# Gathers, scatters and weight subtractions of the GpSimd queue in another order, in an expert stage on one core

## The chip, the cores and the metric

The kernel runs on one core of one Trainium2 chip. The metric is the device time of one execution in microseconds (us); the median of three runs is quoted. Engines are named as in the profile: PE (TensorE, products), DVE (VectorE), ACT (ScalarE), POOL (GpSimd) and SP (SyncE, which only issues DMAs here).

## The reference

A block of a decoder: cross attention of 2048 tokens (8 x 256, width 256) over 120 context rows each, gated and added, then a mixture of 8 experts where each token goes to the one expert with the highest router logit.

```python
x = x + tanh(g_xattn) * xattn(layernorm(x), ctx)          # softmax attention
h = layernorm(x)                                           # (8, 256, 256)
e_of = argmax(h @ router_w.T, axis=-1)
for e in range(8):                                         # I = 704
    mask = (e_of == e)[..., None]
    xe = where(mask, h, 0)
    ye = (silu(xe @ gate_w[e].T) * (xe @ up_w[e].T)) @ down_w[e].T
    out = out + where(mask, ye, 0)
x = x + tanh(g_ffn) * out
```

## The kernel before

It has two stages. The first (to about 72 us) does the attention for eight batches, writes the rows to a table in DRAM (`x1_rows`), routes every token and sorts the tokens by expert. The second is the expert stage. For expert j the tokens' rows are fetched by indirect DMAs (gathers) into a seat in SBUF, in blocks of 128 tokens: two full blocks always (`FULL` = 2), a third block of 80 only if the expert has more than 256 tokens. Here experts 1, 3, 5 and 6 have a third block. After the work the result rows are sent by indirect DMAs (scatters) to their places in `out`. There are five seats and gathers run two experts ahead (`AHEAD` = 2).

Weights are float32 and each product is done in three passes with numbers split in a high and a low part. SP loads the raw weights (`load_gu` L436 for gate and up, `load_d` L443 for down). ACT makes the high part (L728, called by `split_gu` L854 and `split_d` L861). POOL subtracts it from the raw weights to get the low part: `low_gu` (L521) with one L528 for each of two halves c = 0 and 1 and one L529 for a tail, and `low_d` (L531) with one L537. `low_gu(j)` waits for ACT's split of expert j (`a_hg`) and ends in the signal `p_lg`, `low_d(j)` in `p_ld`. SP's next load into the same room (two rooms of raw weights) waits for `p_lg` or `p_ld`, and PE waits for `p_lg` before an expert's first product and for `p_ld` before its down products.

PE does for expert j: six chunks q of gate and up products (L1147, a half chunk first), then transposes the next expert's tokens (L1125), then the down products (L1180). For each chunk ACT takes the gate product and makes the silu (L839, L841), DVE multiplies it with the up product (L1460, L1462), ACT makes the high part (L850, L852) and DVE the low part (L1469, L1471). The up product of chunk q waits for the low part of chunk q - 3 of the same bank, and that stands on DVE behind the multiplication of the next chunk (L1460), which waits for PE's signal of that chunk's up product. ACT normalises gathered rows (L815) and copies PE's transposes (L823). DVE adds a finished block of the output to its seat (L1482, signals `v_out`, `v_out3`), which a scatter waits for.

The order of POOL's queue is written out by hand. `gather(j)` (L604) issues the two full blocks (`fetch`, L578), reads the token count of expert j and issues the third block under a condition; `scatter(j)` (L617) does the same with `send` (L587). Two gathers stand ahead of `low_gu(2)` and `low_d(2)`; then each round j issues `gather(j + 2)`, `low_gu(j + 2)`, `low_d(j + 2)` and `scatter(j - 1)` (L624 to L636). Since `scatter(j - 1)` ends one round and `gather(j + 3)` begins the next, four to six indirect DMAs stand next to each other.

Of the kernel before, what the change touches and what calls it, by code (L numbers as in the profile page):

```python
# [24 lines left out]
F32 = mybir.dt.float32  # L25
# [4 lines left out]
ALU = mybir.AluOpType  # L30
# [7 lines left out]
E, I = 8, 704  # L38
C = H // P
# [8 lines left out]
SPLIT = 3  # L48
# [7 lines left out]
FULL = BL - 1  # L56
# [4 lines left out]
SEATS = 5  # L61
AHEAD = 2
# [7 lines left out]
def flamingo_moe(nc, x, ctxT, g_x, g_f, WqT, WkT, Wv, bv, WrT, Wgu, Wd, WdL, out):  # L70
    with ExitStack() as stack:
# [108 lines left out]
        def raw_of(j, c):  # L180

            return raw_gu[:, j % RAW, 2 * I * c:2 * I * (c + 1)].rearrange("p (o s n) -> p s o n", o=2, s=2)
# [5 lines left out]
        def halves(j, w_part, c):  # L188

            start = start_of(j, w_part, c)  # L190
            both_sides = wgu[:, start:start + 2 * SIDE].rearrange("p (s i) -> p s i", s=2)
            return both_sides[:, :, 0:I].rearrange("p s (o n) -> p s o n", o=2)

        def tails(j, w_part):

            start = start_of(j, w_part, 0)
            return wgu[:, start:start + C * ROW].rearrange("p (c n) -> p c n", c=C)[:, :, I:SIDE]

        def raw_tails(j):

            return raw_gu[:, j % RAW].rearrange("p (c n) -> p c n", c=C)[:, :, 2 * I - LAST:2 * I]
# [74 lines left out]
        a_hg, a_hd = sem("a_hg"), sem("a_hd")  # L276
        p_lg, p_ld = sem("p_lg"), sem("p_ld")
# [220 lines left out]
        def _(pool):  # L498
# [19 lines left out]
            pool.iota(iota_t[:].rearrange("p a b -> p (a b)"), pattern=[[1, NTOK]], base=-NTOK, channel_multiplier=0, **fl).then_inc(k_pool, 1)  # L518
            pool.iota(bounds[:].rearrange("p a b -> p (a b)"), pattern=[[G, MORE]], base=G, channel_multiplier=0, **fl).then_inc(k_pool, 1)

            def low_gu(j, pieces):  # L521

                pool.wait_ge(a_hg, j + 1)
                for c in range(C):
                    raw, hi, lo = raw_of(j, c), halves(j, 0, c), halves(j, 1, c)
                    for n in range(pieces):
                        where = (slice(None), n // 2, n % 2) if pieces > 1 else slice(None)
                        pool.tensor_tensor(lo[where], raw[where], hi[where].bitcast(F32), ALU.subtract)  # L528
                pool.tensor_tensor(tails(j, 1), raw_tails(j), tails(j, 0).bitcast(F32), ALU.subtract).then_inc(p_lg, 1)  # L529

            def low_d(j, pieces):  # L531

# [68 lines left out]
                    third(pool, "pool", sizes[r], lambda: pool.wait_ge(d_scat[r], 16 * BL),  # L601
                          lambda: pool.wait_ge(d_scat[r], 16 * FULL))

            def gather(j):  # L604

                r = j % SEATS
                if j >= SEATS:
                    third(pool, "pool", sizes[j - SEATS], lambda: pool.wait_ge(d_scat[r], 16 * BL),
                          lambda: pool.wait_ge(d_scat[r], 16 * FULL))
                for k in range(FULL):  # L610
                    fetch(j, k, d_gath[r][k])
                if j == 0:
                    pool.wait_ge(v_used, 1)
                sizes.append(count(pool, j))
                third(pool, "pool", sizes[j], lambda: fetch(j, FULL, d_rest[r]))

            def scatter(j):  # L617

                for k in range(FULL):
                    send(j, k, d_scat[j % SEATS])  # L620
                third(pool, "pool", sizes[j], lambda: send(j, FULL, d_scat[j % SEATS]))

            sizes = []
            for j in range(AHEAD):  # L624
                gather(j)
            low_gu(SPLIT - 1, 1)
            low_d(SPLIT - 1, 1)
            for j in range(E):
                if j + AHEAD < E:
                    gather(j + AHEAD)  # L630
                if SPLIT <= j + AHEAD < E:
                    low_gu(j + AHEAD, 1)
                    low_d(j + AHEAD, 1)
                if j:
                    scatter(j - 1)
            scatter(E - 1)  # L636


            def run(j):
# [961 lines left out]
```

## Time and profile before

| | us |
|---|---|
| median of three runs | 213.82 (213.01 to 213.95) |
| profiled execution, span from first to last instruction | 217.2 |
| PE busy | 190.9 |
| POOL busy | 134.8 |
| ACT busy | 116.1 |
| DVE busy | 112.6 |
| mean granted clock of PE over the span | 0.913 |

The profiled execution is one run of its own. A row of a timeline has the start of an instruction in us from the start of the span, its duration, the engine, the line of the kernel, the operation, what it writes and reads, how many instructions are merged in it, and in brackets how long its engine sat idle before and what ended that. A row in which several instructions are merged covers short gaps between them.

### The profile page before, as it was taken

What the parts mean: (1) busy time and instruction counts of PE and PEld (TensorE: products, weight loads), DVE (VectorE), ACT (ScalarE), POOL (GpSimd) and SP (SyncE); (2) the same over time, 40 slices, a digit from 0 to 9 for tenths busy, and PEclk for the clock granted to TensorE, in tenths of its full rate; (3) what the DMA queues carried; (4) which work ended last, traced back from release to release, by engine and by line L of the source; (5) the groups of instructions that cost most, each with busy time, mean ns of one, the idle gap of its engine ahead of it and who ended that gap; (6) DMA issues with size and microseconds to landing.
All of it is one profiled execution on the core that took longest, in us unless ns stands there. A gap on an engine that the chain in (4) does not pass through costs nothing.

```text
span 217.2 us, 4417 instructions
## 1 busy us (share of the span) xinstructions
PE 190.9 (88%) x1365; PEld 173.5 (80%) x1365; DVE 112.6 (52%) x362; ACT 116.1 (53%) x260; POOL 134.8 (62%) x140
## 2 busy tenths in 40 slices
PE   7899999996869697949999998699899699999980
PEld 3566899985668287949999997699799699899970
DVE  2588899976347413623654651551572552563640
ACT  1377778765137123636973984653796740641510
POOL 3002717959354589834998988998987996203111
PEclk9999999998558757997999999799999879999996
DMA  6999451394530126940095185067001101100001
GB/s 180 342 373 394 178 194 49 88 349 172 185 132 0 40 75 177 368 129 0 5 325 187 28 291 200 14 251 255 20 3 65 50 3 67 34 3 27 28 6 49
DMA packets 11710, 28.98 MB, mean 133 GB/s; under 512 B 1928, under 2 KB 8537, under 8 KB 10646
## 3 DMA queue, kind: packets, MB, share of 16 engines
q1 hardware_dynamic: 6320, 20.20, 26.8%
q0 software_dynamic: 1920, 4.53, 6.5%
q10 hardware_dynamic: 3430, 3.74, 4.9%
q8 instruction: 23, 0.38, 0.7%
q14 instruction: 17, 0.14, 0.2%
HBM read 24.26 MB, written 4.52 MB: 132 GB/s over the span
## 4 chain that ended last, share of the span: by engine, by line
PE 76%; DVE 7%; issue 4%; ACT 4%; DMA 4%; another core or an unknown queue 2%; ACTq 1%; POOL 0%; DVEq 0%; POOLq 0%
PE ps L1147 30%; PE ps L1180 19%; PE ps L1008 4%; DMA both<-in_ctxT 4%; PE ps L1029 3%; PE ps L947 3%; PE ps L988 3%; PE ps L977 3%; PE ps L1018 2%; PE ps L1113 2%; PE ps L1098 2%; PE ps L968 2%; PE ps L1125 1%; DVE ps L1460 1%
## 5 line engine op out<-in xcount | busy, mean ns | idle before, releaser
L1147 PE MATMUL ps<-xhT,wgu 128*128 128x256 f32 (+2 forms) x528 | 74.1, 301 | 7.5 <-DVE hT L1471 4.9
L1147 PEld LDWEIGHTS ps<-xhT,wgu 128*128 128x128 f32 x528 | 71.3, 200 | 9.7 <-DVE hT L1471 5.6
L528 POOL TENSOR_TENSOR wgu<-raw_gu,wgu 128x352 fp32r<-128x352 f32 (+1 forms) x28 | 52.8, 1917 | 14.4 <-ACT wgu L728 14.3
L1180 PE MATMUL ps<-wd,hT 128*128 128x256 f32 (+1 forms) x340 | 44.1, 289 | 3.0 <-DVE hT L1469 3.0
L1180 PEld LDWEIGHTS ps<-wd,hT 128*128 128x128 f32 (+1 forms) x340 | 42.3, 187 | 3.5 <-DVE hT L1469 3.4
L1460 DVE TENSOR_TENSOR ps<-V,ps 128x336 f32<-128x336 f32 x40 | 20.4, 511 | 33.8 <-PE ps L1147 24.0
L587 POOL DMA_INDIRECT out<-xin,table x20 | 19.6, 982 | 26.8 <-DVE xin L1482 23.3
L537 POOL TENSOR_TENSOR wd<-both,wd 128x512 fp32r<-128x512 f32 (+1 forms) x12 | 28.6, 2396 | 2.3 <-ACT wd L728 2.3
L839 ACT ACTIVATE V<-ps 128x336 f32<-128x336 f32 x40 | 17.9, 448 | 19.8 <-PE ps L1147 19.5
L578 POOL DMA_INDIRECT xin<-x_rows,table x20 | 19.5, 977 | 9.9 <-issue 5.6
L728 ACT ACTIVATE wgu<-raw_gu 128x704 fp32r<-128x704 f32 (+2 forms) x34 | 24.0, 771 | 1.2 <-issue 1.2
L1482 DVE SCALAR_TENSOR_TENSOR xin<-ps,tg,xin 128x256 f32<-128x256 f32 (+1 forms) x20 | 9.0, 480 | 27.3 <-PE ps L1180 25.1
L1469 DVE TENSOR_TENSOR hT<-ps,hT 128x336 fp32r<-128x336 f32 x40 | 20.0, 501 | 0.4
L850 ACT ACTIVATE hT<-ps 128x336 fp32r<-128x336 f32 x40 | 17.8, 446 | 0.8 <-DVE ps L1460 0.5
L841 ACT ACTIVATE V<-ps 64x336 f32<-64x336 f32 x8 | 3.5, 443 | 26.0 <-PE ps L1147 26.0
L815 ACT ACTIVATE A<-xin,stat 128x256 f32<-128x256 f32 (+1 forms) x20 | 11.8, 594 | 6.3 <-issue 6.3
L396 POOL TENSOR_TENSOR nwt<-nwt 128x8 f32<-128x8 f32 (+1 forms) x6 | 1.4, 232 | 21.9 <-DVE nwt L390 21.6
L728 ACT ACTIVATE wd<-both 128x768 fp32r<-128x768 f32 (+1 forms) x13 | 12.8, 988 | 0.5 <-DMA both<-in_WdL 0.5
L1029 PEld LDWEIGHTS ps<-wrc,wkT 128*128 128x128 f32 x64 | 9.4, 225 | 3.6 <-ACT wkT L725 3.6
L1029 PE MATMUL ps<-wrc,wkT 128*128 128x8 f32 x64 | 10.0, 284 | 1.4 <-ACT wkT L725 1.4
L1008 PE MATMUL ps<-V,pT 120*128 120x256 f32 x32 | 9.4, 420 | 1.8 <-ACT pT L719 1.8
L725 ACT ACTIVATE wkT<-ps 128x512 f32<-128x512 f32 x8 | 4.8, 599 | 11.2 <-PE ps L1018 11.2
(148 smaller groups left out, 248.2 us busy)
## 6 DMA issues: line engine op xcount, KB each, us to landing
raw_gu<-in_Wgu SPq DMA_DIRECT2D x8, 1408.0 KB, 8.6
both<-in_Wd SPq DMA_DIRECT2D x8, 640.0 KB, 4.3
x_rows<-x ACTq DMA_DIRECT2D x8, 256.0 KB, 3.5
xin<-in_x SPq DMA_DIRECT2D x7, 256.0 KB, 9.5
both<-in_WdL SPq DMA_DIRECT2D x16, 64.0 KB, 4.3
both<-in_ctxT ACTq DMA_DIRECT2D x2, 480.0 KB, 8.4
xin<-x_rows,table POOLq DMA_INDIRECT x20, 3.0
out<-xin,table POOLq DMA_INDIRECT x20
```

What stands on the lines that cost most here:

```text
L528: pool.tensor_tensor(lo[where], raw[where], hi[where].bitcast(F32), ALU.subtract)
L537: ins = pool.tensor_tensor(wd[:, j % SPLIT, some, 1, :], raw[:, some, :], wd[:, j % SPLIT, some, 0, :].bitcast(F32), ALU.subtract)
L578: pool.indirect_dma_start(out=seat(j, k), out_offset=None, in_=rows, in_offset=bass.IndirectOffsetOnAxis(ap=index(j, k), axis=0)).then_inc ...
L587: pool.indirect_dma_start(out=out, out_offset=bass.IndirectOffsetOnAxis(ap=index(j, k), axis=0), in_=seat(j, k), in_offset=None, bounds_ch ...
L728: return act.activation(dst, src, ACT.Copy)
L839: act.activation(sg[:, q % 2, :], ps[:, gate_bank(q), 0:G], ACT.Silu).then_inc(a_sg, 1)
L1008: last = pe.matmul(ps[:, 4, H * k:H * k + H], pT[:, P * k:P * k + P], V[0:K, i, :], start=True, stop=True)
L1029: last = pe.matmul(ps[:, 5, E * k:E * k + E], x1T[:, c, P * k:P * k + P], wrc[:, c, :], start=(c == 0), stop=(c == C - 1))
L1147: last = pe.matmul(ps[:, bank, 0:n], weights(j, w_part, c, i, kind), xhT[:, j % 2, x_part, c, 0:n], start=(c == 0 and (w_part, x_part) == ...
L1180: last = pe.matmul(y_of(j, k), hT[:, h_part, some], wd[:, j % SPLIT, i, w_part, :], start=(s == 0 and n == 0 and (k % 2 == 0 or j == E - 1 ...
L1460: dve.tensor_tensor(up, sg[:, q % 2, :], up, ALU.mult).then_inc(v_h, 1)
L1469: dve.tensor_tensor(hT[:, 2 * i + 1, :], h, hT[:, 2 * i, :].bitcast(F32), ALU.subtract).then_inc(v_hT, 1)
```

## The change

POOL's order in the expert stage becomes another. `low_gu` is taken apart in `low_gu_chunk(j, c, pieces)`, one half c at a time, the tail and the signal `p_lg` with the last. `gather` and `scatter` are each taken apart in a part for the two full blocks and one for the third. In a round, the full gathers, the first half of the subtraction, the full scatters, the second half, the third-block gather, the third-block scatter and the subtraction of the down weights follow each other. Also, the full gathers of expert 2 go between `low_gu(2)` and `low_d(2)`. No other engine's program changes.

```diff
+            def low_gu_chunk(j, c, pieces):
+
+                pool.wait_ge(a_hg, j + 1)
...
+                if c == C - 1:
+                    pool.tensor_tensor(tails(j, 1), raw_tails(j), tails(j, 0).bitcast(F32), ALU.subtract).then_inc(p_lg, 1)
...
-            def gather(j):
+            def gather_full(j):
...
                 for k in range(FULL):
                     fetch(j, k, d_gath[r][k])
+
+            def gather_rest(j):
+
                 if j == 0:
                     pool.wait_ge(v_used, 1)
                 sizes.append(count(pool, j))
-                third(pool, "pool", sizes[j], lambda: fetch(j, FULL, d_rest[r]))
-
-            def scatter(j):
+                third(pool, "pool", sizes[j], lambda: fetch(j, FULL, d_rest[j % SEATS]))
+
+            def scatter_full(j):
 
                 for k in range(FULL):
                     send(j, k, d_scat[j % SEATS])
+
+            def scatter_rest(j):
+
                 third(pool, "pool", sizes[j], lambda: send(j, FULL, d_scat[j % SEATS]))
 
             sizes = []
             for j in range(AHEAD):
-                gather(j)
-            low_gu(SPLIT - 1, 1)
+                gather_full(j)
+                gather_rest(j)
+            low_gu_chunk(SPLIT - 1, 0, 1)
+            low_gu_chunk(SPLIT - 1, 1, 1)
+            gather_full(AHEAD)
             low_d(SPLIT - 1, 1)
-            for j in range(E):
-                if j + AHEAD < E:
-                    gather(j + AHEAD)
-                if SPLIT <= j + AHEAD < E:
-                    low_gu(j + AHEAD, 1)
-                    low_d(j + AHEAD, 1)
-                if j:
-                    scatter(j - 1)
-            scatter(E - 1)
+            gather_rest(AHEAD)
+            for j in range(1, E - AHEAD):
+                gather_full(j + AHEAD)
+                low_gu_chunk(j + AHEAD, 0, 1)
+                scatter_full(j - 1)
+                low_gu_chunk(j + AHEAD, 1, 1)
+                gather_rest(j + AHEAD)
+                scatter_rest(j - 1)
+                low_d(j + AHEAD, 1)
+            for j in range(E - AHEAD - 1, E):
+                scatter_full(j)
+                scatter_rest(j)
```

## Rows read from the trace of the kernel before

**Rows 1.** The page: busy time of PE, and its two costliest groups of instructions.

```profile
PE 190.9 (88%) x1365; PEld 173.5 (80%) x1365; DVE 112.6 (52%) x362; ACT 116.1 (53%) x260; POOL 134.8 (62%) x140
L1147 PE MATMUL ps<-xhT,wgu 128*128 128x256 f32 (+2 forms) x528 | 74.1, 301 | 7.5 <-DVE hT L1471 4.9
L1180 PE MATMUL ps<-wd,hT 128*128 128x256 f32 (+1 forms) x340 | 44.1, 289 | 3.0 <-DVE hT L1469 3.0
```

**Rows 2.** Engines by stretch: experts 1 and 5.

```profile
core 0: us, PE busy (x) PEld busy (x) DVE busy (x) ACT busy (x) POOL busy (x), PEclk, DMA share, GB/s
101.80:116.40 14.60, 14.60 (x122) 14.56 (x121) 8.17 (x17) 10.48 (x22) 13.33 (x8) 1.00 0.49 172
164.60:183.50 18.90, 16.99 (x125) 16.55 (x124) 8.31 (x18) 8.62 (x20) 16.29 (x11) 0.91 0.14 43
```

**Rows 3.** Timeline of the expert stage, PE's rows, all but one behind idle time.

```profile
97.34 4.51 PE L1180 MATMUL ps<-wd,hT 128*128 128x256 f32 x23 [3.02 <-DVE hT L1469]
129.20 5.68 PE L1147 MATMUL ps<-xhT,wgu 128*128 128x336 f32 x36
137.48 4.74 PE L1147 MATMUL ps<-xhT,wgu 128*128 128x336 f32 x19 [2.61 <-DVE hT L1471]
153.35 6.50 PE L1147 MATMUL ps<-xhT,wgu 128*128 128x256 f32 x48 [0.45 <-ACT V L841]
171.30 4.97 PE L1147 MATMUL ps<-xhT,wgu 128*128 128x272 f32 x25 [1.90 <-DVE hT L1471]
188.39 4.06 PE L1147 MATMUL ps<-xhT,wgu 128*128 128x272 f32 x30 [0.38 <-DVE hT L1471]
```

**Rows 4.** Engines by stretch, columns as above: a slow and a full window of PE's clock.

```profile
97.60:101.00 3.40, 3.40 (x18) 3.40 (x18) 0.92 (x3) 3.03 (x5) 0.03 (x1) 0.50 0.00 0
102.00:105.40 3.40, 3.40 (x29) 3.40 (x28) 2.29 (x5) 2.47 (x6) 3.40 (x2) 1.00 0.02 5
```

**Rows 5.** Timeline at the end of expert 0: transposes, last gather, ACT and DVE.

```profile
92.23 0.60 PE L1125 MATMUL ps<-ident,A 128*128 128x128 f32 x4
94.08 0.90 POOL L578 DMA_INDIRECT xin<-x_rows,table  x1 [0.30 <-issue]
96.35 0.60 ACT L823 ACTIVATE xhT<-ps 128x512 fp32r<-128x512 f32 x1 [2.16 <-remote]
96.36 0.51 DVE L1460 TENSOR_TENSOR ps<-V,ps 128x336 f32<-128x336 f32 x1 [4.18 <-remote]
```

**Rows 6.** Timeline of experts 3, 5 and 6: last DMAs of runs, DVE behind them.

```profile
136.38 0.51 DVE L1460 TENSOR_TENSOR ps<-V,ps 128x336 f32<-128x336 f32 x1 [4.19 <-PE ps L1147]
...
166.88 2.30 PEld L1147 LDWEIGHTS ps<-xhT,wgu 128*128 128x128 f32 x18 [0.23 <-issue]
167.97 0.97 POOL L578 DMA_INDIRECT xin<-x_rows,table  x1 [0.30 <-issue]
170.20 0.51 DVE L1460 TENSOR_TENSOR ps<-V,ps 128x336 f32<-128x336 f32 x1 [2.82 <-PE ps L1147]
...
187.29 0.51 DVE L1460 TENSOR_TENSOR ps<-V,ps 128x336 f32<-128x336 f32 x1 [1.98 <-PE ps L1147]
```

**Rows 7.** Timeline of POOL: the subtractions, and its wait before expert 3's.

```profile
100.97 3.24 POOL L528 TENSOR_TENSOR wgu<-raw_gu,wgu 128x1408 fp32r<-128x1408 f32 x1 [5.99 <-ACT wgu L728]
168.97 6.35 POOL L528 TENSOR_TENSOR wgu<-raw_gu,wgu 128x1408 fp32r<-128x1408 f32 x2
175.69 3.50 POOL L537 TENSOR_TENSOR wd<-both,wd 128x1536 fp32r<-128x1536 f32 x1
```

**Rows 8.** Timeline: runs of DMAs that cost PE little, and the work behind them.

```profile
117.57 0.48 DVE L1482 SCALAR_TENSOR_TENSOR xin<-ps,tg,xin 80x256 f32<-80x256 f32 x1 [2.07 <-PE ps L1180]
202.56 0.45 ACT L839 ACTIVATE V<-ps 128x336 f32<-128x336 f32 x1 [1.43 <-PE ps L1147]
```

**Rows 9.** Timeline of SP and ACT: a load, its split; the page: time to landing.

```profile
107.89 0.33 SPq L441 DMA_DIRECT2D raw_gu<-in_Wgu  x1
126.55 3.03 ACT L728 ACTIVATE wgu<-raw_gu 128x704 fp32r<-128x704 f32 x5 [0.26 <-issue]
raw_gu<-in_Wgu SPq DMA_DIRECT2D x8, 1408.0 KB, 8.6
```

More of the change, by code:

```diff
@@ L519, in _ @@
             pool.iota(bounds[:].rearrange("p a b -> p (a b)"), pattern=[[G, MORE]], base=G, channel_multiplier=0, **fl).then_inc(k_pool, 1)
+            def low_gu_chunk(j, c, pieces):
+                pool.wait_ge(a_hg, j + 1)
+                raw, hi, lo = raw_of(j, c), halves(j, 0, c), halves(j, 1, c)
+                for n in range(pieces):
+                    where = (slice(None), n // 2, n % 2) if pieces > 1 else slice(None)
+                    pool.tensor_tensor(lo[where], raw[where], hi[where].bitcast(F32), ALU.subtract)
+                if c == C - 1:
+                    pool.tensor_tensor(tails(j, 1), raw_tails(j), tails(j, 0).bitcast(F32), ALU.subtract).then_inc(p_lg, 1)
             def low_gu(j, pieces):
-                pool.wait_ge(a_hg, j + 1)
                 for c in range(C):
[L525 to L529, printed above, removed]
+                    low_gu_chunk(j, c, pieces)
             def low_d(j, pieces):
```

## The prediction, made before the changed kernel was run

> **What bounds the kernel now.** I read the page first. TensorE (PE) is busy 191 of 217.2 us, and the two products of the expert stage, L1147 and L1180, carry 118 us of it [rows 1]. So a change on GpSimd (POOL) can move the end only by what it does to PE. I then took the expert stage in stretches, one per expert [rows 2]. Expert 1 (three blocks of tokens) takes 14.6 us with PE never idle. Expert 5, of the same width (272 columns) and the same number of products, takes 18.9, with 1.9 us of PE idle and part of the stretch below full clock. The stage is PE's, but it holds holes, and the holes are what the change could touch.
>
> The timeline of PE alone gives them: 3.02, 2.61, 0.45, 1.90 and 0.38 us before L1180 or L1147 [rows 3]. They add up to 8.4 us. After the three long ones PE's granted clock is 0.50 for 3.4 us (1.2 instead of 2.4 GHz); after the short ones it is not. The slow window behind the first hole starts 18 products, a full one 29 [rows 4], so it loses 11/29 of 3.4 us = 1.3 us; three such windows (from 97.6, 138.5 and 172.7 us) lose 3.9. The stage's removable loss is 8.4 + 3.9 = 12.3 us.
>
> What causes the holes is seen on the engines that PE waits for. At the end of expert 0 PE finishes its transposes at 92.83; ScalarE's copy of them (L823), which needs only that signal and has its engine free from 94.19, starts at 96.35, and VectorE's L1460 starts at 96.36 after 4.18 us of idle [rows 5]. In expert 5 the next 18 weight loads begin at 166.88, so the first 18 are over and the product that L1460 wants is done soon after, by about 167.2 (an estimate); L1460 starts at 170.20, idle for 2.82 us. In expert 3 it is idle for 4.19 us [rows 6]. So signals from PE reach ScalarE and VectorE one and a half to four microseconds late. All three lie in or behind a run of five or six indirect DMAs on POOL, 1.25 to 1.3 us apart (0.9 to 1.0 us each and 0.30 us of issue), and the late work starts 1.3 to 1.4 us after the last DMA's row ends: 94.98 to 96.35, 168.94 to 170.20 [rows 5, 6]. Outside these runs the same waits are short; that is where expert 1 has its unbroken 14.6 us. That the DMAs hold the signals up is inferred from this timing; the trace has no row for the holding itself.
> The Trainium skill (Perfetto Trace Analysis, "DMA Instruction — SWDGE (GPSIMD)") says that the row of such a DMA ends when its last descriptor is written, not when the data has moved. The rows agree: the effect outlasts the DMA's row.
>
> How much lateness PE bears follows from pairs of rows: VectorE's idle 4.19, 2.82 and 1.98 us goes with PE idle 2.61, 1.90 and 0.38 [rows 3, 6]. About 1 to 1.6 us of waiting is covered by the products already released; what is beyond reaches PE.
>
> **The change part by part.** It removes and adds no data instruction. The 20 gathers, 20 scatters, 12 large subtractions (L528, one per half of an expert's gate and up weights) and the rest stay; there are a few more conditional branches on POOL (the third-block test of a gather and of a scatter are apart). Their price has no row; the nearest is the issue idle of 0.30 us before a DMA, which has such code in it. Six more at 0 to 0.3 us is 0 to 1.8 us on POOL, off PE's path; I take 0.5.
>
> 1. Runs are cut. For experts 3 to 7 the order is now: two gathers, half a subtraction (6.35/2 = 3.2 us), two scatters, the other half with its tail, then at most one third-block gather and one scatter, then the subtraction for the down weights (3.50) [rows 7]. No run is longer than two, except where a third-block gather of expert 2 would stand (expert 2 has none here). The runs of five and six that stood at experts 0, 3, 4 and 5 are gone. Of the five scatters in expert 6 the two of scatter 4 leave, three stay.
>
> 2. What a pair still costs. The nearest rows from above: the gather at 167.97 closed a run of five, and PE lost 1.90 us and a slow window (1.3), 3.2 in all [rows 3, 6]. From below: the run of two scatters and two gathers in expert 2 left DVE idle 2.07 us before L1482 and PE not at all; the three scatters at 201 us left L839 idle 1.43 us and PE not at all; the scatters of expert 6 cost 0.38 us; the run of five at the start of expert 4 cost 0.45 [rows 3, 8]. So the four cheap runs cost 0, 0, 0.38 and 0.45: I take 0.3 for a pair, which is nearest to runs of two to four. Eleven pairs lie among the subtractions (gathers of experts 2 to 7, scatters of 0 to 4): 3.3 us. For slow windows I take half of one, 0.7. Ends: 0 and 11 x 3.2 = 35.
>
> 3. What is moved. Gathers of expert 2 go ahead of the down subtraction of expert 2, which ends 2.5 us later (two DMAs at 1.26). SP's load of the down weights of expert 4 waits for it, and the load of gate and up weights of expert 5 stands behind that in SP's queue, but waits for POOL's later subtraction anyway (107.89) [rows 9]. ScalarE wants expert 4's down weights only in expert 2, 25 us on. Nothing is late.
> In each later round the gate and up subtraction is stretched by the two scatters in its middle, 2.6 us, and by what lies ahead of it, up to 4 us in all. Behind its signal stand SP's loads two experts on (L441), which land in 8.6 us: for expert 5, issued at 107.89, landed by 116.5, wanted by ScalarE (L728) at 126.55, so 10 us of cover [rows 9]. The change takes 2.6 to 4 of these. If PE also comes 9 us earlier late in the stage, nothing may be left for expert 7; a load 2 us late would stop ScalarE, and PE bears 1 to 1.6 of it, so 0 to 1 us: I take 0. PE wants the subtracted weights of expert 3 at 129.20 [rows 3], and they are ready when SP's load is let go, at 107.89, so 21 us are left for a delay of 2.6.
> Behind the wait of a scatter (v_out) now stands the second half of the subtraction. On the old clock POOL would come to scatter 0 at 100.97 + 3.2 = 104.2, and PE's down products of expert 0 end at 97.34 + 4.51 = 101.85 [rows 3, 7], so VectorE has added them by then; both come earlier together, and for later experts POOL is further behind. POOL sits idle for 5.99 us ahead of L528 at 100.97, waiting for ScalarE's split [rows 7], which itself was held up by the late signal at 96.35; without it POOL starts up to 4.8 us earlier. Third-block gathers come later by half a round; that of expert 6 goes out 3.2 + 2.6 + 3.7 = 9.5 us behind the full ones and is wanted in mid-expert 5, which is near it if PE is 9 us early: 0 to 2 us late, of which 1 is covered; I take 0.
> 4. The end stays: PE's last L1180, VectorE's L1482, the last scatter.
>
> Sum on the profiled execution: 217.2 - 12.3 + 3.3 + 0.7 = 208.9 us of span. The median of the runs shown is 213.82, 3.4 below that span, a ratio of 0.984; 208.9 x 0.984 = 205.6. I forecast **205.5 us**. Should the 3.4 us be holes that only a profiled execution has, 12.3 becomes 8.9 and the time is 213.8 - 8.9 + 4.0 = 208.9.
>
> **Rivals.**
> - Part of the gain: pairs still meet the tender places. Where one falls between PE's second up-product of an expert and VectorE's L1460, it costs the full 3.2 us. Two such places on top: 205.5 + 6.4 = 211.9; one: 208.7. For it: the two gathers that end expert 5's run stood right on such a place. I take 208.7 to 212.7 us, at 210.5.
> - Slower, by spreading: each pair catches a signal of its own, since there are now two runs in an expert where there was one. At 3.2 us for each, the old loss of 12.3 is made up by four of the eleven pairs; six give 217.2 - 12.3 + 19.2 = 224.1 of span, about 220.5 us. It decides from the fourth hit on. Against it: four of the seven runs of before cost 0 to 0.45 us, though they have three to five DMAs.
> - Nothing: the lateness hangs on the number of DMAs or on the weight loads in flight (the runs of experts 0, 2 and 3 lie beside SP's loads), not on the run's length. Then the holes move about and their sum stays: 213.8 us. Against it: expert 5's run had hardly a weight load beside it (43 GB/s over the stretch, 172 in expert 1) and still cost 1.90 [rows 2, 3].
> The Trainium skill (DMA: Bandwidth & Descriptors, "Issuing engines are not separate DMA queues") says that DMAs of all issuers run on the same 16 engines and interleave. By that the spacing on POOL would matter only through load, and this rival's time is what it gives. The trace speaks against it, as far as it goes, in expert 5.
> - All of it: pairs cost nothing, 217.2 - 12.3 = 204.9 of span, 201.6 us.
>
> **How the numbers follow.** Forecast (202.5 to 208.7) 0.48; part of it 0.20; all of it (under 202.5) 0.09; nothing 0.10; slower 0.13. About 0.5% (1.1 us) is what a measurement of this kernel can tell from no change. Faster by more is 0.48 + 0.20 + 0.09 = 0.77, within 0.10, slower 0.13. The range reaches from 199.5 to 214.0: it leaves out the slower case and little below. The forecast's own range is 202.5 to 208.7.
>
> **What would show it.** Right: POOL's timeline has no three L578 or L587 in a row before the last scatters; PE's gaps of 3.02, 2.61 and 1.90 us are gone; at most one slow window between 82 us and the end of the stage; expert 5's stretch near 15 us; VectorE's waits before L1460 under 2 us; expert 1 unchanged. Wrong in step 2: new PE gaps of 1 to 2 us, each 1.3 us behind a pair, and slow windows after them. Wrong in step 3: ScalarE idle before L728 for a DMA, or PE waiting for POOL. Wrong in the cause: PE's signals late with no DMA of POOL near.

## The result, and the profile after

| | before | after |
|---|---|---|
| median of the timed runs, us | 213.41 (211.28 to 213.95, 4 runs) | 199.23 (196.86 to 201.60, 4 runs) |
| ratio after / before | | 0.928, 95% interval 0.915 to 0.940 |
| span of the profiled execution | 217.2 | 198.4 |
| first to last product of the expert stage | 82.85 to 210.95: 128.1 | 80.09 to 190.9: 110.8 |
| PE idle in the expert stage | 8.7 | 0.0 |
| slow windows of PE's clock in it | 4 | 0 |

The changed kernel is 14.2 us faster; the forecast said 8.3. The measured time lies just under the whole range (199.5 to 214.0) and 3.3 us under the forecast's own (202.5 to 208.7). The sign and the place were right, the size was not. Medians here are over all executions, while a ratio and its interval compare only each kernel's undisturbed (fast) ones, so a ratio can differ a little from the quotient of two medians.

The page of the kernel after: span, PE's busy time, its clock in 40 slices of 5 us, and PE's two large groups, as in [rows 1].

```profile
span 198.4 us, 4417 instructions
...
PE 181.0 (91%) x1365; PEld 165.6 (83%) x1365; DVE 112.8 (57%) x362; ACT 116.0 (58%) x260; POOL 136.2 (69%) x140
...
PEclk9999999999985976999999999999999999999995
...
L1164 PE MATMUL ps<-xhT,wgu 128*128 128x256 f32 (+2 forms) x528 | 67.2, 287 | 1.8 <-DVE xhT L1460 1.8
...
L1197 PE MATMUL ps<-wd,hT 128*128 128x256 f32 (+1 forms) x340 | 42.6, 283 | 0.1
```

The lines have moved by up to 17: L1164 was L1147, L1197 was L1180, L1477 was L1460, L1499 was L1482; L583 and L592 are the gather and the scatter (L578 and L587). PE's idle time before the up and gate products was 7.5 us and is 1.8, all of it before the very first product of the stage; before the down products it was 3.0 and is 0.1. From slice 17 to slice 39, which hold the expert stage (80 to 191 us), the clock shows nothing below 9. The two groups also take 8.4 us less busy time with the same number of products (74.1 to 67.2 and 44.1 to 42.6); most of that is the slow windows gone, as the comparison below shows.

The same by stretches (columns as in [rows 2]): inside experts 1, 3 and 5 of the kernel after.

```profile
core 0: us, PE busy (x) PEld busy (x) DVE busy (x) ACT busy (x) POOL busy (x), PEclk, DMA share, GB/s
92.80:107.40 14.60, 14.60 (x122) 14.48 (x121) 8.10 (x17) 10.58 (x22) 13.81 (x8) 1.00 0.35 124
120.10:136.50 16.40, 16.40 (x122) 16.38 (x121) 8.02 (x17) 10.75 (x23) 15.28 (x10) 1.00 0.51 172
148.90:163.50 14.60, 14.54 (x120) 14.34 (x119) 8.20 (x18) 8.19 (x20) 13.47 (x9) 1.00 0.13 32
```

PE is busy without a break of 0.1 us in all three at clock 1.00. Expert 5 took 18.9 us at 0.91 before [rows 2]; it takes 15.2 now, nearly as little as expert 1.

Worked out from PE's timelines, the time of each expert in us:

| expert | 0 | 1 | 2 | 3 | 4 | 5 | 6 | 7 |
|---|---|---|---|---|---|---|---|---|
| before | 18.8 | 14.7 | 12.8 | 21.0 | 14.3 | 18.9 | 15.4 | 12.2 |
| after | 12.5 | 14.8 | 12.4 | 16.6 | 12.4 | 15.2 | 14.7 | 12.3 |
| gain | 6.4 | -0.1 | 0.4 | 4.4 | 1.9 | 3.7 | 0.7 | -0.1 |

The three experts that held the long holes of [rows 3] give 14.5 of the 17.3 us. PE's 904 rows of the stage (products and transposes) stand in both traces in the same order, so the time from each one's start to the next one's can be compared one by one. Of the 17.3 us, 10.1 lie at eight products that PE had to wait for, 0.7 at the products right behind these, 5.9 in the four slow windows (1.5 each), and 0.5 is left. The rows show less idle time than the 10.1 us (8.7) because a product's row overlaps the next one's: it is 0.28 us long where the next starts after 0.12.

The rest of the difference in span, 18.8 - 17.3 = 1.5 us, is no work of the change: the stage began 2.8 us earlier, and from the start of the last scatter's row to the end of the span it took 6.2 us and not 5.0. Over the profiles of all the kernels below, the stage begins between 80.4 and 84.1 us and this tail takes 4.7 to 6.3. The slow window at 83.9 us is chance too: five of the profiles below have one in expert 0 with PE never idle before it in the stage, one of them (plain, chip E) without an indirect DMA in the expert stage. That leaves 15.8 us of the 17.3 for the change.

POOL's timeline in one round of the kernel after (gathers for expert 5, scatters of expert 2), and VectorE's multiplications behind the two pairs:

```profile
123.46 1.01 POOL L583 DMA_INDIRECT xin<-x_rows,table  x1 [0.16 <-issue]
124.77 0.96 POOL L583 DMA_INDIRECT xin<-x_rows,table  x1 [0.30 <-issue]
125.75 3.25 POOL L527 TENSOR_TENSOR wgu<-raw_gu,wgu 128x1408 fp32r<-128x1408 f32 x1
129.17 1.02 POOL L592 DMA_INDIRECT out<-xin,table  x1 [0.17 <-issue]
130.49 1.00 POOL L592 DMA_INDIRECT out<-xin,table  x1 [0.30 <-issue]
131.49 3.25 POOL L527 TENSOR_TENSOR wgu<-raw_gu,wgu 128x1408 fp32r<-128x1408 f32 x1
134.69 0.46 POOL L529 TENSOR_TENSOR wgu<-raw_gu,wgu 128x128 fp32r<-128x128 f32 x1
135.32 0.94 POOL L583 DMA_INDIRECT xin<-x_rows,table  x1 [0.16 <-issue]
136.26 3.56 POOL L542 TENSOR_TENSOR wd<-both,wd 128x1536 fp32r<-128x1536 f32 x1
...
122.78 0.51 DVE L1477 TENSOR_TENSOR ps<-V,ps 128x336 f32<-128x336 f32 x1 [0.93 <-PE ps L1164]
126.45 0.51 DVE L1477 TENSOR_TENSOR ps<-V,ps 128x336 f32<-128x336 f32 x1 [0.79 <-PE ps L1164]
```

The longest run of DMAs in the loop is two; three scatters in a row stand only behind it (at 173.0 and 178.7 us). VectorE waits 0.79 us behind the first pair, where it waited 4.19 behind the run in expert 3 before [rows 6].

### The profile page after: what moved, and what is told of

Read it like the earlier page. It is cut to its first block, busy times and chain, and to the rows that moved or that the text cites. A ratio compares the mean times of both kernels' runs of the same rounds, so it can differ in the third digit from the quotient of the medians.

```text
span 198.4 us, 4417 instructions
## 1 busy us (share of the span) xinstructions
PE 181.0 (91%) x1365; PEld 165.6 (83%) x1365; DVE 112.8 (57%) x362; ACT 116.0 (58%) x260; POOL 136.2 (69%) x140
## 4 chain that ended last, share of the span: by engine, by line
PE 49%; POOL 19%; issue 13%; DMA 5%; ACT 5%; DVE 4%; POOLq 1%; ACTq 1%; DVEq 0%
PE ps L1164 12%; POOL wgu L527 9%; PE ps L1197 8%; POOL out L592 5%; PE ps L1115 4%; DMA both<-in_ctxT 4%; PE ps L1025 4%; PE ps L964 3%; PE ps L1005 3%; POOL xin L583 3%; PE ps L1046 3%; PE ps L994 3%; PE ps L1130 2%; POOL wd L542 2%; ACT wgu L745 2%
## 5 line engine op out<-in xcount | busy, mean ns | idle before, releaser
L1164 PE MATMUL ps<-xhT,wgu 128*128 128x256 f32 (+2 forms) x528 | 67.2, 287 | 1.8 <-DVE xhT L1460 1.8
L1164 PEld LDWEIGHTS ps<-xhT,wgu 128*128 128x128 f32 x528 | 66.2, 188 | 2.2 <-issue 2.2
L527 POOL TENSOR_TENSOR wgu<-raw_gu,wgu 128x352 fp32r<-128x352 f32 (+1 forms) x28 | 53.3, 1927 | 10.7 <-ACT wgu L745 10.6
L1197 PE MATMUL ps<-wd,hT 128*128 128x256 f32 (+1 forms) x340 | 42.6, 283 | 0.1
L1197 PEld LDWEIGHTS ps<-wd,hT 128*128 128x128 f32 (+1 forms) x340 | 40.7, 180 | 0.6 <-DVE hT L1486 0.5
L1477 DVE TENSOR_TENSOR ps<-V,ps 128x336 f32<-128x336 f32 x40 | 20.5, 512 | 22.3 <-PE ps L1164 13.7
L592 POOL DMA_INDIRECT out<-xin,table x20 | 19.7, 984 | 15.4 <-DVE xin L1499 11.6
L583 POOL DMA_INDIRECT xin<-x_rows,table x20 | 19.6, 982 | 7.7 <-issue 4.5
L1499 DVE SCALAR_TENSOR_TENSOR xin<-ps,tg,xin 128x256 f32<-128x256 f32 (+1 forms) x20 | 9.0, 480 | 22.2 <-PE ps L1197 22.2
L745 ACT ACTIVATE wd<-both 128x768 fp32r<-128x768 f32 (+1 forms) x13 | 12.8, 987 | 0.1
L1046 PEld LDWEIGHTS ps<-wrc,wkT 128*128 128x128 f32 x64 | 8.1, 199 | 3.3 <-ACT wkT L742 3.3
L1046 PE MATMUL ps<-wrc,wkT 128*128 128x8 f32 x64 | 8.8, 264 | 1.4 <-ACT wkT L742 1.4
L1025 PE MATMUL ps<-V,pT 120*128 120x256 f32 x32 | 8.5, 387 | 1.5 <-ACT pT L736 1.5
```

What stands on the lines that cost most here:

```text
L583: pool.indirect_dma_start(out=seat(j, k), out_offset=None, in_=rows, in_offset=bass.IndirectOffsetOnAxis(ap=index(j, k), axis=0)).then_inc ...
L592: pool.indirect_dma_start(out=out, out_offset=bass.IndirectOffsetOnAxis(ap=index(j, k), axis=0), in_=seat(j, k), in_offset=None, bounds_ch ...
L745: return act.activation(dst, src, ACT.Copy)
L1046: last = pe.matmul(ps[:, 5, E * k:E * k + E], x1T[:, c, P * k:P * k + P], wrc[:, c, :], start=(c == 0), stop=(c == C - 1))
L1164: last = pe.matmul(ps[:, bank, 0:n], weights(j, w_part, c, i, kind), xhT[:, j % 2, x_part, c, 0:n], start=(c == 0 and (w_part, x_part) == ...
L1197: last = pe.matmul(y_of(j, k), hT[:, h_part, some], wd[:, j % SPLIT, i, w_part, :], start=(s == 0 and n == 0 and (k % 2 == 0 or j == E - 1 ...
```

## The experiments

The theory: a long unbroken run of indirect DMAs on POOL delays PE's signals to ScalarE and VectorE. Its rivals: the lateness hangs on where the DMAs fall in a round, not on the length of the run; on their number, bytes or on traffic; any work of that length in the queue does it; or the gain is not the loop's but the beginning's, where gathers of expert 2 were moved. The runs lay on five further chips, called B to F, each used on one occasion only, so "chip" below always means that chip on that occasion. A stands for the result above; the record does not name its chip. "Before" is timed again on each, and only kernels of one chip are compared by ratio. In the edits `gf`, `gr` stand for `gather_full(j + AHEAD)` and `gather_rest(j + AHEAD)`, `sf`, `sr` for `scatter_full(j - 1)` and `scatter_rest(j - 1)`, `c0`, `c1` for the two halves of the subtraction, `d` for `low_d(j + AHEAD, 1)`. The loop of after is then gf c0 sf c1 gr sr d.

### Chip B: the length of the run, and its place

The kernel before unchanged, for its holes:

> The kernel before, unchanged, profiled once more. Its first profile had a span of 217.2 us with PE holes of 8.4 us in the expert stage and reached that stage 2.8 us later than the changed kernel, though nothing ahead of the stage was changed. If the holes belong to the kernel, this profile has again 7 to 11 us of PE idle in the expert stage at the same places (behind the runs of five and six indirect DMAs at experts 0, 3, 5) and slow clock windows behind them. If they are chance, they stand elsewhere or are gone and the span is under 208 us. The start of the expert stage tells whether the 2.8 us are chance: near 80 us in one of the repeats if so, 82.9 if not.

Measured: 212.73 us beside 215.44 for the kernel before in the same set, 1.002 (0.987 to 1.016), as it has to be. In its profile PE is idle for 5.3 us in the stage, with two slow windows. The last gather of a run of six in expert 3, VectorE's next multiplication, and PE behind it (timeline):

```profile
129.81 0.90 POOL L578 DMA_INDIRECT xin<-x_rows,table  x1 [0.30 <-issue]
131.97 0.51 DVE L1460 TENSOR_TENSOR ps<-V,ps 128x336 f32<-128x336 f32 x1 [4.11 <-PE ps L1147]
133.07 2.23 PE L1147 MATMUL ps<-xhT,wgu 128*128 128x336 f32 x7 [2.32 <-DVE hT L1471]
```

This is the pattern of [rows 3, 6] again: VectorE 4.11 us late, released 1.3 us after the last DMA's row ends, and PE idle for 2.32.

Runs of three:

```diff
 gf
+gr
 c0
 sf
-c1
-gr
 sr
+c1
 d
```

> The changed kernel with the third-block gather and scatter back with their full ones: rounds of gathers (2 or 3), half a subtraction, scatters (2 or 3), other half, down subtraction. Runs of three where there were two. Theory of the run's length: signals of PE are held for as long as a run lasts beyond its first DMA or two, and 1 to 1.6 us are covered, so runs of three cost little: 0 to 2 us more than the changed kernel, 197 to 202 us. Theory of the place: the runs stand where the pairs stood, so the time is that of the changed kernel as well, 197 to 201. They part in the two other kernels of this set; if this one is above 205 a single DMA more is what counts.

Measured: 202.64 us, ratio 0.942 (0.916 to 0.968). PE idle 0.5 us; the stage takes 113.3. Of these, 1.5 us are a slow window in expert 0, without idle time before it.

Runs of four, the scatters directly ahead of the gathers:

```diff
+sf
 gf
 c0
-sf
 c1
 gr
 sr
 d
```

> The changed kernel with the full scatters moved ahead of the full gathers, so that each round has a run of four, then both halves of the subtraction with nothing between, then the third blocks and the down subtraction. Theory of the run's length: four in a row cost between nothing (two scatters and two gathers in expert 2 of the kernel before) and the 1.9 us and more of the runs of five; I expect 1 to 3 holes, 202 to 208 us. Theory of the place: the runs stand near the places of the changed kernel's gather pairs, clear of PE's tender ones, so 198 to 201 us.

Measured: 207.64 us, 0.973 (0.939 to 1.008). PE idle 3.1 us, the stage takes 115.9. The last gather of a run of four, VectorE behind it, and PE (timeline):

```profile
116.87 0.97 POOL L583 DMA_INDIRECT xin<-x_rows,table  x1 [0.30 <-issue]
117.49 0.51 DVE L1477 TENSOR_TENSOR ps<-V,ps 128x336 f32<-128x336 f32 x1 [2.64 <-PE ps L1164]
118.60 2.60 PE L1164 MATMUL ps<-xhT,wgu 128*128 128x256 f32 x17 [1.40 <-issue]
```

VectorE is held for 2.64 us and PE loses 1.40. Here VectorE came free during the last DMA and not behind it.

All DMAs of a round in one run, but half a round away from where they stood:

```diff
-gf
 c0
 sf
-c1
-gr
 sr
+gf
+gr
+c1
 d
```

> The full run of the kernel before (scatters and gathers, five or six in a row) kept whole, but put between the two halves of the subtraction. Theory of the run's length: it holds PE's signals just as before, for 3 to 4 us a run, so most of the loss stays: 207 to 216 us, with PE idle 1.5 to 3 us behind three or more of the five runs. Theory of the place: the loss came from where the runs met PE's chain; half a round away they cost a third or less of it, 198 to 204 us.

Measured: 217.37 us, 1.019 (0.990 to 1.048). PE is idle for 8.5 us. The first and last of a run of six, VectorE behind it, and PE's own row (timelines):

```profile
149.99 1.01 POOL L592 DMA_INDIRECT out<-xin,table  x1 [0.17 <-issue]
...
156.44 0.90 POOL L583 DMA_INDIRECT xin<-x_rows,table  x1 [0.30 <-issue]
158.63 0.51 DVE L1477 TENSOR_TENSOR ps<-V,ps 128x336 f32<-128x336 f32 x1 [5.59 <-remote]
...
159.61 4.89 PE L1197 MATMUL ps<-wd,hT 128*128 128x256 f32 x26 [3.45 <-DVE hT L1486]
```

The run went elsewhere and took its hole with it: other experts pay now (4: 18.0 us, 1: 17.1, 2: 14.6), the sum is the old one. So the place does not decide, the length does, and on this one chip it grows in steps: three in a row 202.6 us, four 207.6, five and six 212.7 to 217.4. The single executions of the four kernels hardly meet: 200.4 to 203.9, 206.2 to 210.1, and 209.1 to 220.5 for those with five and six. Two in a row were not timed here; 199.2 us on chip A is the nearest.

### Chip C: each part alone, and a surprise

The loop in its old order with the new beginning:

```diff
 gf
+gr
 c0
-sf
 c1
-gr
-sr
 d
+sf
+sr
```

> The changed kernel with its loop put back: in each round gathers, both halves, the down subtraction, then the scatters, so that runs of four to six stand at the places of the kernel before; only the gathers of expert 2 stay ahead of its down subtraction. Theory of the run's length: nearly the whole loss comes back, 207 to 214 us, with holes of 1.5 us and more behind the runs in experts 3 and 5; gone is only the hole of 3.0 us at the end of expert 0. Theory of the place is silent here, since the places are the old ones.

The old beginning with the new loop:

```diff
 low_gu_chunk(SPLIT - 1, 0, 1)
 low_gu_chunk(SPLIT - 1, 1, 1)
-gather_full(AHEAD)
 low_d(SPLIT - 1, 1)
+gather_full(AHEAD)
 gather_rest(AHEAD)
```

> The changed kernel with its beginning put back: gathers of experts 2 and 3 are one run of four ahead of expert 3's subtraction (before: five); the loop stays as changed. By the run's length the hole at the end of expert 0 (3.0 us in one profile of the kernel before, 0.1 in the other) may come back, 0 to 3 us, and the rest is as in the changed kernel: 199 to 204 us. Together with the kernel whose loop is put back this splits the gain: I expect over three quarters of it from the loop.

One DMA at a time: each full gather and scatter alone, a quarter of the subtraction behind it, the third blocks apart around `d`:

```diff
-gf
-c0
-sf
-c1
+gather block 0, quarter 0
+gather block 1, quarter 1
+scatter block 0, quarter 2
+scatter block 1, quarter 3
 gr
-sr
 d
+sr
```

> Every full gather and scatter stands alone, with a quarter of the subtraction (1.6 us) between it and the next; POOL's work is the same but for a few more instructions. In the changed kernel PE has no idle time of 0.1 us or more in the expert stage. If that is all there is to gain, this one is as fast, 197 to 202 us, PE bound all through. If single DMAs still held up something that the idle time does not show, it is faster by 1 to 3 us. If it is the length of the gaps between DMAs and not their number in a row that matters, gaps of 1.6 us may be too short and holes of 0.5 to 2 us come back, 202 to 207 us.

Plain DMAs of the same size in the order of before; they copy rows in sequence instead of the sorted ones, and the third blocks go to a spare table:

```diff
-pool.indirect_dma_start(out=seat(j, k), ..., in_=rows, in_offset=...)
+pool.dma_start(seat(j, k), rows[at:at + BLOCK[k], :])
...
-pool.indirect_dma_start(out=out, out_offset=..., in_=seat(j, k), ...)
+pool.dma_start(room, seat(j, k))
```

> The kernel before with the 40 gathers and scatters of its expert stage as plain copies of the same size, issued by POOL at the same places (rows in order, not by the table, so tokens and experts do not belong together; third blocks are written to a spare room). Theory that any DMA whose descriptors POOL writes holds up PE's signals: the holes stay, 206 to 214 us, PE idle over 4 us. Theory that it is the indirection (one address for each row): the holes are gone, 196 to 203 us, and POOL's rows for the DMAs are as long or shorter.

| chip C | us | ratio to before | PE idle in the stage | stage |
|---|---|---|---|---|
| before | 201.98 (198.84 to 204.21) | | | |
| loop undone | 203.69 | 1.020 (1.010 to 1.030) | 0 | 112.1 |
| beginning undone | 202.15 | 1.009 (0.991 to 1.027) | 0 | 110.4 |
| single | 206.05 | 1.032 (1.018 to 1.046) | 1.6 | 112.8 |
| plain | 200.39 | 1.003 (0.978 to 1.028) | 0 | 110.2 |

The expectation for the loop undone missed (207 to 214 us), and the others were met for no reason of theirs, since the kernel before itself takes 202 us on this chip, 11 to 13 less than on A or B. The kernel with the loop undone has its runs of five and six, and PE is never idle: the holes are absent although their supposed cause is there. So these runs tell nothing about the parts of the change, and they were repeated on another chip below. In its profile the loop undone is 1.7 us longer in the stage than the beginning undone, and 1.5 of that is a slow window at 84.8 us in expert 0 (14.0 us, not 12.5), behind no hole; why its median is 1.7 us above that of the kernel before stays open.

The single DMAs show a cost that doesn't need late signals: the third-block gather goes out later still. In expert 4 ScalarE waits for the third block of expert 5, and PE for ScalarE to transpose it (timeline):

```profile
148.01 0.60 ACT L852 ACTIVATE A<-xin,stat 80x256 f32<-80x256 f32 x1 [3.10 <-DMA xin<-x_rows,table]
148.76 0.33 PE L1173 MATMUL ps<-ident,A 80*128 80x80 f32 x2 [0.98 <-ACT A L852]
```

ScalarE loses 3.10 us and PE 0.98; expert 4 takes 14.9 us, 2.5 more than with the beginning undone. Spacing the DMAs finer than pairs had nothing to gain on this chip and ran into this. On a chip with holes it was not run.

### Chip D: before and after side by side where there are no holes

> The changed kernel, unchanged, once more, beside the kernel before. The last set ran on another chip, on which the kernel before took 202 us and the kernel with its loop put back had no hole at all in the expert stage. So the holes seem to belong to the chip as well as to the runs of DMAs. Theory that the change only cures the holes: where the kernel before takes 212 us or more, this one takes 197 to 202; where the kernel before takes about 202, the two are within 1% of each other. Theory that the changed order is also faster by itself: it is 3 us or more faster on either chip.

> The kernel before, unchanged, for a profile on the chip of this set. On a chip where it takes 212 us or more: PE idle 4 to 9 us in the expert stage, behind runs of five and six. On a chip where it takes about 202: no hole of 0.1 us or more, a stage of 110 to 113 us, and the same runs of DMAs on POOL at the same spacing.

Half the rows in each gather and scatter, the number and order of the DMAs as before (the other half of the tokens is not moved):

```diff
-out=seat(j, k), ..., ap=index(j, k)
+out=seat(j, k)[0:BLOCK[k] // 2], ..., ap=index(j, k)[0:BLOCK[k] // 2]
```

> The kernel before with every gather and scatter cut to the first half of its rows (64 of 128, 40 of 80); the other rows are neither fetched nor written. The count of DMAs, their places and the runs stay. On a chip with holes: if the number of DMAs in a row is the cause, 206 to 214 us and holes as before; if it is the descriptors or bytes that they carry, holes shrink by half or more, 198 to 205 us. On a chip without holes: 198 to 203 us, which tells nothing of them.

> The kernel before with plain copies in place of the gathers and scatters (as in the last set; it took 200.4 us there, where the kernel before took 202.0 and the holes were missing for all kernels). On a chip with holes: any DMA whose descriptors POOL writes, 206 to 214 us; only the indirect ones, 196 to 203 us. On a chip without holes it tells nothing new: 199 to 202 us.

| chip D | us | ratio to before | PE idle in the stage | stage |
|---|---|---|---|---|
| before | 202.32 (199.89 to 204.94) | | | |
| before, profiled (again2) | 201.46, one run | | 0 | 110.2 |
| after | 202.58 (200.06 to 204.14) | 1.010 (0.998 to 1.022) | 0 | 110.5 |
| half the rows | 202.82 | 1.004 (0.997 to 1.010) | 0 | 111.9 |
| plain | 201.31 | 0.991 (0.979 to 1.003) | 0 | 110.4 |

On this chip the change does nothing that can be told: the interval, -0.2 to +2.2%, holds both nothing and a small loss. The profile of the kernel before, expert 3 (timeline): PE at work, VectorE, and the last gather of the run of six.

```profile
122.51 8.75 PE L1147 MATMUL ps<-xhT,wgu 128*128 128x336 f32 x56
...
125.54 0.51 DVE L1460 TENSOR_TENSOR ps<-V,ps 128x336 f32<-128x336 f32 x1 [0.93 <-PE ps L1147]
127.38 0.51 DVE L1460 TENSOR_TENSOR ps<-V,ps 128x336 f32<-128x336 f32 x1 [0.79 <-PE ps L1147]
...
128.04 0.90 POOL L578 DMA_INDIRECT xin<-x_rows,table  x1 [0.30 <-issue]
```

It is the same place as on chip B, with the same DMAs 1.2 to 1.3 us apart and the same 0.90 us row. VectorE waits 0.93 and 0.79 us where it waited 4.11, which is what the kernel after shows on A. The stage takes 110.2 us, and 110.5 with the new order: PE's own time.

The same changed kernel is profiled on A and on D, so its waits can be set side by side. Behind pairs no signal of PE is more than some 0.3 us later on A. Behind the two runs of three scatters it is; VectorE's rows on A, and the same two on D:

```profile
177.36 0.88 DVE L1499 SCALAR_TENSOR_TENSOR xin<-ps,tg,xin 128x256 f32<-128x256 f32 x2 [2.90 <-PE ps L1197]
183.08 0.51 DVE L1477 TENSOR_TENSOR ps<-V,ps 128x336 f32<-128x336 f32 x1 [1.10 <-PE ps L1164]
...
176.89 0.88 DVE L1499 SCALAR_TENSOR_TENSOR xin<-ps,tg,xin 128x256 f32<-128x256 f32 x2 [2.30 <-PE ps L1197]
182.46 0.51 DVE L1477 TENSOR_TENSOR ps<-V,ps 128x336 f32<-128x336 f32 x1 [0.35 <-PE ps L1164]
```

So the changed kernel's profile on A comes from a chip that holds signals up, 0.60 and 0.75 us here, and its short runs still cost PE nothing.

### Chip E: the parts and the kind of DMA, on a chip with holes

The four kernels of chips C and D that mattered, sent again (edits as above).

> The changed kernel with its loop put back, once more, for a chip with holes. There (kernel before at 209 us or more) by the run's length: 206 to 214 us, PE idle 3 to 8 us behind the runs of five and six. On a chip without holes: within 2% of the kernel before, about 203 us, no idle time.

> The changed kernel with its beginning put back, once more, for a chip with holes. There: one run of four ahead of expert 3's subtraction, 0 to 3 us of idle at the end of expert 0 and none later, 199 to 205 us. On a chip without holes: about 202 us.

> The kernel before with plain copies issued by POOL in place of gathers and scatters, once more, for a chip with holes. If every DMA whose descriptors POOL writes does it, 206 to 214 us and PE idle over 3 us; if only indirect ones, 196 to 204 us and idle under 1 us. On a chip without holes 199 to 203 us.

> The kernel before with gathers and scatters cut to the first half of their rows (the others are not moved), once more, for a chip with holes. POOL's rows for them were hardly shorter (0.92 instead of 0.98 us), so the runs last as long. If the number of DMAs is the cause: 206 to 214 us, idle over 3 us; if what they move: 198 to 205 us, idle under 2 us. On a chip without holes 200 to 204 us.

| chip E | us | ratio to before | PE idle in the stage | stage |
|---|---|---|---|---|
| before | 215.54 (212.98 to 219.66) | | | |
| loop undone | 214.07 (212.32 to 216.91) | 0.985 (0.971 to 1.000) | 6.8 | 122.6 |
| beginning undone | 204.81 (204.43 to 205.08) | 0.946 (0.937 to 0.956) | 0.7 | 112.7 |
| plain | 203.13 (2 runs) | 0.939 (0.926 to 0.951) | 0 | 111.8 |
| half the rows | 215.36 (207.68 to 218.58) | about 1, no interval | 8.5 | 124.1 |

The loop undone, PE's two longest holes:

```profile
130.49 4.88 PE L1164 MATMUL ps<-xhT,wgu 128*128 128x336 f32 x30 [2.35 <-DVE hT L1488]
...
146.23 4.03 PE L1164 MATMUL ps<-xhT,wgu 128*128 128x256 f32 x20 [2.30 <-ACT V L858]
```

They are back, with nearly the time of before (expert 3 takes 19.4 us, expert 4 16.4). The beginning undone leaves one run of four, at the end of expert 0: its last gather, ScalarE's copy behind it (L840, the L823 of [rows 5]), and PE.

```profile
92.18 0.94 POOL L583 DMA_INDIRECT xin<-x_rows,table  x1 [0.30 <-issue]
92.69 0.60 ACT L840 ACTIVATE xhT<-ps 128x512 fp32r<-128x512 f32 x1 [2.02 <-remote]
...
95.69 1.53 PE L1164 MATMUL ps<-xhT,wgu 128*128 128x272 f32 x9 [0.23 <-issue]
```

ScalarE is held for 2.02 us, but PE loses only 0.23: a late signal that work already released covers. So the gain is the loop's: with the new loop alone the time falls by 10.7 us, with the new beginning alone by 1.5. The whole change was not timed on this chip. Against the stage of the changed kernel on A (110.8 us) this one's 112.7 leaves the beginning 1.9 us at the most. Only 0.23 of the 0.7 us of idle lie behind the run of four, so the later, short runs are not wholly free here.

Half the rows, the last gather of the run in expert 5, ScalarE and PE behind it:

```profile
162.76 0.91 POOL L578 DMA_INDIRECT xin<-x_rows,table  x1 [0.30 <-issue]
164.97 0.45 ACT L839 ACTIVATE V<-ps 128x336 f32<-128x336 f32 x1 [3.89 <-remote]
165.47 2.78 PE L1147 MATMUL ps<-xhT,wgu 128*128 128x272 f32 x17 [2.22 <-ACT V L839]
```

With half the rows and bytes the DMA's row still takes 0.91 us, and the hole stays. PE's idle time adds up to 8.5 us, with no slow window in the stage. Plain DMAs, two scatters and three gathers of one run:

```profile
136.20 1.10 POOL L594 DMA_DIRECT2D out<-xin  x2
137.30 1.60 POOL L581 DMA_DIRECT2D xin<-x_rows  x3
```

Five of them take 2.7 us in place of the 5.9 of the run of five with half the rows (157.77 to 163.67), 0.55 and 0.53 us each with no issue time between, and not one of PE's signals is late. So the bytes of the gathers and scatters are out, and so is a run of any DMAs of this count. What these runs don't part is indirection itself from the length of the run in time: the plain run is both plain and short.
The Trainium skill (DMA: Bandwidth & Descriptors, "Issuing engines are not separate DMA queues") says that the DMAs of all issuers share the same 16 engines and interleave. Here half the bytes of gathers and scatters changed nothing (215.36 us), and plain DMAs of the full size at the same places left no signal late (203.13), so load on the shared engines does not explain the late signals.

### Chip F: gathers or scatters

One kind plain, the other indirect:

> The kernel before with its gathers as plain copies by POOL (rows in order, so the tokens are not the expert's) and its scatters as they are. On a chip with holes (kernel before at 209 us or more): if each kind holds up PE's signals, runs of two or three scatters are left and cost 0 to 3 us over the 203 us of plain copies for both, 203 to 206; if scatters alone do it, 208 to 214. On a chip without holes 200 to 204 us.

> The kernel before with its scatters as plain copies by POOL (rows in order, third blocks to a spare room) and its gathers as they are. On a chip with holes: if each kind holds up the signals, runs of two or three gathers are left, and 203 to 206 us; if gathers alone do it, 208 to 214. On a chip without holes 200 to 204 us.

Measured: 201.62 us (1.006, 0.999 to 1.014) and 201.45 beside 201.65 for the kernel before. On this chip the kernel before takes 202 us and both profiles show no idle PE, so the question was not answered: whether gathers or scatters hold the signals stays open.

## Why the prediction was right and where it failed

- **PE bounds, and only its holes can go.** Right. In the three profiles of chips A and D in which PE is never idle the stage takes 110.2 to 110.8 us with either order.
- **The cause, a run of indirect DMAs.** It was inferred from timing alone, and the runs of chips B and E confirm it: by length (3, 4, 5 and more on B: 202.6, 207.6, 213 to 217 us), by place (half a round away, still 217.4), by kind (plain, 203.1). What was not foreseen is that it needs a chip that has it.
- **What a pair still costs, 4.0 us (3.3 and 0.7): the step that failed.** On A it is 0: PE is never idle in the stage. I took 0.3 us a pair as nearest to the runs of [rows 3, 8], which had three to five DMAs. The price was read from longer runs and spread evenly over short ones, while it rises from the third or fourth DMA on. The trace of before had a pair nearly by itself: two scatters from 179.35 to 181.67 us, the next 1.2 us later, and PE without idle time until 188.02.
- **Removable loss, 12.3 us: mis-sized.** It measured 17.3 in the stage. The holes were read as 8.4 us of idle rows; by the starts of the products they delayed PE by 10.1, and by 0.7 more at the products right behind. The slow windows were priced at 1.3 us each by counting products of different widths; each cost 1.5, in this pair and in the profiles where expert 0 takes 14.0 us with a window and 12.5 without. And there were four, not three: the one at 83.9 was left out as not standing behind a hole, rightly, and went by chance. So 10.8 + 5.9 stand for 8.4 + 3.9, and 0.5 is left.
- **What is moved, priced at 0.** Right as a sum: ScalarE never waits for the loads of the stage. How fast they land on A is not known. The 8.6 us of [rows 9] and the 9.2 of the page after are medians of four loads whose landing the trace has, all of them issued before 56 us, ahead of the stage; on D two loads of the stage land in 6.3 and 7.1 us. ScalarE waits for other data once, for 1.1 us before 155.54, for a third-block gather, and PE works on. The risk named for the third-block gather (0 to 2 us) is real: one step further apart it cost ScalarE 3.10 us and PE 0.98.
- **From the profiled span to the median, x 0.984: wrong, and lucky.** An execution's device time is 1.7 to 1.9 us above its span in every run here (200.11 and 198.4, for one). The profiled execution of before thus took about 218.9 us, 5 over its median. That surplus was in the profile I read, and a ratio does not take it out. Where it lay is not shown; the stage's late start (2.8) and the window at 83.9 (1.5) come to most of it.
- The sum: in spans, forecast 208.9 and measured 198.4, so 10.5 us too high: 4.0 for the pairs, 5.0 for the removable loss, 1.5 outside the stage. In medians only 6.3 is missing (205.5 and 199.2), because the scaling took off 3.4 us where the measured median lies 0.8 above the span. That error of 4.2 us hid part of the others.
- **The rivals.** "All of it" (201.6) came nearest and had a chance of 0.09; I had kept it low because the pairs' upper end was read from a run of five. "Slower by spreading" fell: no pair on A made PE wait. "Nothing" is what chip D showed, and C and F, where before is as fast, leave no holes to remove either; but not for its reason: there was no lateness to begin with.
- **The signs.** No three in a row in the loop, the three holes gone, expert 5 near 15 us (15.2), expert 1 unchanged (14.7 and 14.8): all as said. VectorE's waits for PE before the multiplication are at most 1.1 us; for ScalarE one there reaches 2.1, a little over the 2 named. "At most one slow window": none.

## What to carry to other kernels

Where GpSimd issues many indirect DMAs, put compute of its own between them, two in a row at most, and look for late signals (another engine idle behind a product that is long done) before calling such a run harmless. Spacing them further had no gain where it was tried (chip C) and delayed the gathers themselves. Time both kernels on more than one chip: the same pair gave 0.93 in one set and 1.01 (0.998 to 1.022) on another chip, so the new order is insurance whose price is nothing to 2%.

## What was not expected of the hardware

- One and the same kernel, with the same DMAs at the same spacing, takes 213 to 216 us on chips A, B and E and 202 on C, D and F. The difference is PE's late signals and the slow clock behind them (stage 121.9 us on B, 110.2 on D). Why is open, and since each chip was used once, chip and occasion are not told apart.
- The traces of the two kinds differ in one more thing, by which a reader can tell them. The page gives the median time to landing of the indirect scatters on C and D and none on A, B and E; from again (B) and again2 (D):

```profile
out<-xin,table POOLq DMA_INDIRECT x20
out<-xin,table POOLq DMA_INDIRECT x20, 2.8
```

The traces hold 1,516 to 1,558 marks of DMA completions on C, D and F, and 949 to 1,260 on A, B and E. In after on A the missing ones lie around the indirect DMAs; plain DMAs on E have 1,558. So on these chips marks of completions are lost in the same kernels in which signals are late. Whether they have one cause is not shown. Every execution timed here has a recorded span and clock, so no run tells whether the signals are late without the recording.
- On the first kind the loss is no fixed price of a DMA: with at most two in a row in the loop PE is idle for 0 us (A) and some 0.5 (E, besides the run of four), at three 0.5, at four 3.1, at five and six 5.3 to 8.7. The signals come through 0.9 to 1.4 us after the last DMA's row where the engine waited out the whole run. How they are held is not visible in any row.
- An indirect DMA's row takes 0.96 us (gather) and 0.98 (scatter) in the median of before, 0.91 and 0.93 with half the rows, and a plain one some 0.55.
